# One fused transformer block with a mixture of experts on one core: a block's work spread over four periods instead of three, attention by q times k, a residual added on TensorE

## The reference, cut to what matters

```
x  = attn_q_x                                   # [16, 512, 256]
z  = layernorm(x);  xn = layernorm(z) * ln1_w + ln1_b
q, k, v = xn @ wq + bq, xn @ wk + bk, xn @ wv + bv      # each 16 heads of 16
fq, fk = elu(q) + 1, elu(k) + 1
kv   = einsum('bhnd,bhne->bnde', fk, v)         # per token 16 x 16
qkv  = einsum('bhnd,bnde->bhne', fq, kv)
den  = einsum('bhnd,bnd->bhn', fq, fk.sum(heads))
a    = (qkv / (den + 1e-6)) @ wo + bo;  y = z + a
x1   = x + y + (gelu(layernorm2(y) @ fc_w + fc_b) @ proj_w + proj_b)
t    = layernorm(x1)
top 2 of 8 experts by t @ gate_w.T, weights by softmax
out  = x1 + shared(t) + sum over the two experts of w_e * expert_e(t)
       # shared and each expert: (silu(t @ g) * (t @ u)) @ down, 384 wide
```

## Time and profile before

| | |
|---|---|
| median of 3 runs | 1912.48 us (1909.49 to 1914.32) |
| the profiled execution's own time | 1909.86 us |
| its span | 1908.1 us |
| mean granted TensorE clock in it | 0.935 of full |
| busy over the span: PE, DVE, POOL, ACT | 91%, 67%, 67%, 40% |
| busy from 700 to 800 us: PE, DVE, POOL, ACT | 94.05, 92.16, 88.52, 49.94 us of 100 |

### The profile page before, as it was taken

One profiled execution on the slowest core, in us unless ns is written; L12 is line 12 of the kernel. 1 busy time (PEld: TensorE's weight loads), 2 busy tenths in 40 slices (PEclk: granted clock), 3 DMA queues, 4 the chain that ended last, 5 costly groups with the idle time before them and its releaser, 6 DMA issues.

```text
span 1908.1 us, 25917 instructions
## 1 busy us (share of the span) xinstructions
PE 1739.2 (91%) x7160; PEld 1247.1 (65%) x7161; DVE 1275.3 (67%) x2291; ACT 772.7 (40%) x1518; POOL 1270.5 (67%) x749
## 2 busy tenths in 40 slices
PE   3489998999999999998999899797999999999997
PEld 1255665555656655665566566555888888888886
DVE  7999898988988989889889899613222222222221
ACT  2245455354454453544544534431333322333222
POOL 4877888888888888889888888802333333333333
PEclk8699898898998988989989889888999999999999
DMA  5001110110101101101011010106777777677674
GB/s 188 27 29 44 45 45 23 44 38 28 44 11 44 44 22 44 42 25 44 15 41 44 22 44 34 41 4 187 157 162 163 162 158 157 161 163 164 158 155 90
DMA packets 87130, 148.57 MB, mean 78 GB/s; under 512 B 8640, under 2 KB 71872, under 8 KB 86720
## 3 DMA queue, kind: packets, MB, share of 16 engines
q1 hardware_dynamic: 60512, 112.58, 18.9%
q0 software_dynamic: 26592, 35.67, 11.2%
HBM read 101.79 MB, written 48.56 MB: 79 GB/s over the span
## 4 chain that ended last, share of the span: by engine, by line
PE 47%; POOL 26%; DVE 14%; issue 8%; ACT 3%; DMA 1%; POOLq 0%; DVEq 0%; SPq 0%; ACTq 0%
POOL prod_pool L464 10%; PE p_b L1362 10%; PE p_b L1373 10%; PE p_q L1362 7%; PE p_b L1301 6%; DVE prod L838 4%; POOL prod_pool L537 3%; PE p_v L1362 3%; POOL prod_pool L482 3%; PE p_b L1222 3%; POOL rows_sorted L501 3%; POOL prod_pool L520 3%; DVE prod L863 2%; PE p_b L1270 2%; DVE kvT L846 2%
## 5 line engine op out<-in xcount | busy, mean ns | idle before, releaser
L577 POOL DMA_INDIRECT out_rows<-prod_pool,prod x142 | 220.9, 1555 | 384.3 <-ACT prod_pool L756 353.8
L464 POOL TENSOR_TENSOR prod_pool<-prod_pool 128x544 f32<-128x544 f32 (+4 forms) x240 | 400.0, 1667 | 18.8
L1270 PE MATMUL p_b<-bT,fc_sb 128*128 128x512 f32 x512 | 225.6, 599 | 12.1 <-ACT bT L683 12.1
L1222 PE MATMUL p_b<-proj_sb,hid 128*128 128x256 f32 x1024 | 230.5, 379 | 0.0
L846 DVE TENSOR_REDUCE kvT<-prod 128x128 f32<-128x2048 f32 x96 | 219.5, 2286 | 2.7
L838 DVE TENSOR_TENSOR prod<-p_q,v_dve 128x4096 f32<-128x4096 f32 x48 | 211.9, 4415 | 0.0
L1222 PEld LDWEIGHTS p_b<-proj_sb,hid 128*128 128x128 f32 x1024 | 189.6, 190 | 27.7 <-issue 0.5
L1301 PE MATMUL p_b<-bT,sgup_sb 128*128 128x512 f32 x384 | 206.5, 695 | 0.0
L1362 PE MATMUL p_b<-prod,exp_up 128*128 128x256 f32 x840 | 187.1, 379 | 0.0
L1270 PEld LDWEIGHTS p_b<-bT,fc_sb 128*128 128x128 f32 x512 | 96.5, 191 | 131.8 <-issue 108.1
L876 DVE TENSOR_REDUCE qkv<-prod 128x204 f32<-128x3264 f32 x48 | 170.4, 3550 | 4.0 <-DVE rs_a L808 3.2
(11 more groups left out here) (164 smaller groups left out, 2867.0 us busy)
## 6 DMA issues: line engine op xcount, KB each, us to landing
exp_up<-in_experts SPq DMA_DIRECT2D x71, 768.0 KB, 4.7
prod<-rows_sorted SPq DMA_DIRECT2D x71, 260.0 KB, 2.8
xin<-in_x SPq DMA_DIRECT2D x16, 512.0 KB, 3.4
xres<-in_x SPq DMA_DIRECT2D x16, 512.0 KB, 3.6
out_rows<-x SPq DMA_DIRECT2D x16, 512.0 KB, 3.3
exp_dn<-in_experts SPq DMA_DIRECT2D x8, 384.0 KB, 5.5
out_rows<-prod_pool,prod POOLq DMA_INDIRECT x142, 3.8
rows_sorted<-rows SPq DMA_DIRECT2D x2, 1040.0 KB, 6.7
```

What stands on the lines that cost most here:

```text
L464: done(g.tensor_tensor(prod_pool[:, at:at + n * w], prod_pool[:, at:at + n * w], prod_pool[:, at + n * w:at + 2 * n * w], ALU.add))
L577: pool.indirect_dma_start(out=out[:, :], out_offset=bass.IndirectOffsetOnAxis(ap=tok_i[j][:, a:a + 1], axis=0), in_=yg[j][:, a * D:(a + 1) ...
L1222: ins = t_.matmul(o, src[:, k, t * P:(t + 1) * P], w[:, k, :], start=k == 0, stop=bias_at is None and k == chunks - 1)
L1270: ins = t_.matmul(bnk[:], fc_sb[:, k, f * P:(f + 1) * P], bT[:, k, :], start=k == 0, stop=k == KC - 1)
```

## The change

The pipeline gets a stage more. Under `stages(c)` a body now has `core` (block c, attention), `stage_b` (block c-1: wo, LayerNorm 2, gelu layer), `stage_c` (block c-2: LayerNorm 3, router, shared expert's up products, scatter) and `stage_d` (block c-3: shared down product, store). The program runs periods 0 to 18 instead of 0 to 17. The hardware loop holds two periods a round (c = 4 to 13), because `rows` and `x1` now alternate between two buffers.

- On TensorE the router and the whole shared expert of block c-2 (6 up products, and the down product of c-3) stand ahead of `hT` and the gelu layer of block c-1. The up products use two PSUM banks instead of three.
- Attention first multiplies q with k (scores 16x16 for each token, `products_1`, `sums_1`), sums the scores to the denominator (`totals`), then multiplies scores with v (`products_2`, `sums_2`). Every product has 4096 elements for 16 heads. VectorE does tiles 1 and 3 whole and half of the heads of tile 2; GpSimd tile 0 whole and the other 8 heads of tile 2, in one go (`heads`).
- The scores stay in the tile's q and k bank, and so do denominators and small statistics; `pq_free` for tile 1, 2 and 3 is given after the division, not after the second product. For tile 3 that is after `attn_ready`.
- POOL's addition of `xmid` to `xres` is gone. TensorE adds `xmid` in PSUM by a product with the identity in `to_tokens` (`plus`).
- A few values of four or eight numbers (`first2`, `gap_1`, `shift_c`) pass through PSUM.

The diff, cut to its core: the sizes, TensorE's body from `x3T` to `hT`, the added product, VectorE's two new steps, the first half of VectorE's body, and GpSimd's `heads`.

```
-DVE_HEADS = 12
-POOL_HEADS = HEADS - DVE_HEADS
+SPLIT = 2
+POOL_HEADS = 8
...
             def body(c, j):
...
+                if stage_c:
+                    transpose_block(rows[j % 2], (p_b0, p_b1), x3T_psum,
+                                    lambda t: wait(pe, rows_ready, TPB * (c - 2) + t + 1))
                 if core:
                     project_x(c, 2, "P")
+                if stage_c:
+                    logits(c)
+                if stage_d:
+                    down(c)
                 if stage_b:
+                    if stage_c:
+                        wait(pe, ln2_var, c)
+                        shared_up(c)
+                    if core:
+                        project_x(c, 3, "P")
+                    if stage_c:
+                        ranks(c)
+                        wait(pe, up_taken, 2 * HCH * (c - 1))
                     transpose_block(hnorm, (p_b2, p_b3), hT_psum,
...
+                    if plus is not None:
+                        t_.matmul(o, ident[:], plus[:, t, :], start=False, stop=False)
...
+            def products_1(u):
+                done.sync()
+                n = own_heads(u)
+                done.later(v.tensor_tensor(
+                    prod[:, 0:n * HH].rearrange("p (h g d) -> p h g d", h=n, g=HEADS),
+                    p_qk[u % 2][:, 0:n * HD].rearrange("p (h d) -> p h d", h=n).unsqueeze(2)
+                    .to_broadcast([P, n, HEADS, HD]),
+                    eqk[u % 2][:, D:2 * D].rearrange("p (g d) -> p g d", d=HD).unsqueeze(1)
+                    .to_broadcast([P, n, HEADS, HD]), ALU.mult))
+            def sums_1(u, lo, hi):
+                done.sync()
+                done.later(v.tensor_reduce(
+                    p_qk[u % 2][:, lo * HEADS:hi * HEADS],
+                    prod[:, lo * HH:hi * HH].rearrange("p (a d) -> p a d", d=HD), AX.X, ALU.add))
...
             def body(c, j):
...
                 if core:
+                    features(c, 1)
+                    products_1(1)
+                if stage_c:
+                    shift_3(c)
+                if core:
+                    sums_1(1, 0, half)
+                if stage_b:
+                    residual_1(c)
+                if core:
+                    keep_scales(c)
+                    if more:
+                        ln1_stats(c + 1)
+                if stage_b:
+                    scales_b(ln2_std, ln2_scale, c)
+                if core:
+                    sums_1(1, half, HEADS)
+                    totals(1, den_1[:, 0:HEADS])
+                    products_2(c, 1, False)
+                    if more:
+                        ln1_scales(c + 1)
+                if stage_c:
+                    choose(c, j)
+                if core:
+                    done.sync()
+                    guard(den_1[:, 0:HEADS])
+                    sums_2(1)
+                    inverse(den_1[:, 0:HEADS])
+                    if more:
+                        dve.wait_ge(ln1_scale, c + 2)
+                    wait(dve, attnT_psum, KC * c)
+                    features(c, 2)
+                    done.sync()
+                    done.later(divide(0, 0, qkv[1][:], den_1[:, 0:HEADS]))
+                    if stage_c:
+                        dve.wait_ge(chosen_ready, c - 1)
+                    release(c, 1)
+                    products_1(2)
...
             def heads(c):
+                wait(pool, feat_ready, 4 * c + SPLIT + 1)
+                own = slice(HEADS, HEADS + POOL_HEADS)
+                features = eqk[SPLIT % 2]
+                announce(pool, scores(features[:, (HEADS - POOL_HEADS) * HD:D], by_head(features[:, D:2 * D]), POOL_HEADS),
+                         share_qk_used, c + 1)
+                announce(pool, halve(flat(s_pool[:, own, :])), pool_s, c + 1)
+                announce(pool, mixed(s_pool[:, own, :], v_dve[SPLIT % 2][:].rearrange("p e g -> p g e"),
+                                     POOL_HEADS), share_v_used, c + 1)
+                announce(pool, halve(flat(qkv_pool[:, own, :])), pool_qkv, c + 1)
```

More of the change, by code:

```diff
@@ L383, in body, with store @@
                         sp.dma_start(exp_dn[:, e, :], experts[e, :, EXU:EXW]).then_inc(experts_in, 16)
[L384 to L394, removed]
+                if stage_d and (core or stage_b):
+                    store(c, j)
+            def store(c, j):
+                wait(sp, out_ready, c - 2)
+                sp.dma_start(out_blk[bass.ds(c - 3, 1)].rearrange("b p t d -> p (b t) d"), x1[(j + 1) % 2][:]
+                             ).then_inc(out_stored, 16)
+            periods(sp, body)
             sp.wait_ge(pads_at, 1)
@@ L679, in body @@
                     rsqrt(rs_a[:, 0:2], sq_a[:], ln1_log, ln1_std, c + 2)
+                if stage_c and stage_b:
+                    table(ACT.Silu)
+                    take_shared(c)
+                    table_exp_ln()
+                    wait(act, gap_ready, c - 1)
+                    a.activation(gap_e[:], gap[:], ACT.Exp).then_inc(gap_exp, 1)
+                if core:
+                    take_qkv(c, 3)
                 if stage_b:
@@ L714, in body @@
                 if stage_b:
-                    wait(act, gap_ready, c)
-                    a.activation(gap_e[:], gap[:], ACT.Exp).then_inc(gap_exp, 1)
-                    table(ACT.Silu, 2)
-                    take_shared(c, range(3, 2 * HCH))
+                    scales_3(c)
             act.wait_ge(pool_const, 3)
@@ L730, in _ @@
             take_qkv(0, 1)
[L731 to L736 removed]
+            periods(act, body)
             def take_gT(k, j):
@@ L1050, in body @@
-                if stage_b:
-                    place(c)
-                if core and not last:
-                    done.sync()
-                    dve.sem_inc(pq_free, 1)
-                if stage_b:
-                    weights(c)
+                        dve.sem_inc(pq_free, 1)
             dve.wait_ge(pool_const, 4)
@@ L1227, in to_tokens, with body @@
                         ins.then_inc(ready, 1)
-            def body(c, core, stage_b, tail):
-                more = core and (not isinstance(c, int) or c < BLOCKS - 1)
+            def body(c, j):
+                core, more, stage_b, stage_c, stage_d = stages(c)
                 if core:
```

678 lines of the change are left out of this document (344 added, 334 removed).

## The result

| | before | after |
|---|---|---|
| median | 1911.2 us (1909.49 to 1914.32, 4 runs) | 1930.36 us (1928.72 to 1933.22, 4 runs) |
| ratio | | 1.010, 95% interval 1.008 to 1.012 |
| the profiled execution: own time, span | 1909.86, 1908.1 | 1928.72, 1926.6 |
| mean granted TensorE clock | 0.935 | 0.958 |

The change makes the kernel 1.0% slower. The forecast was 1880 us with 0.75 for faster: wrong in sign, and the range ended at 1930.

A forecast was written before the change was run, and what follows sets the result against it. No engine full: a ring of waits from TensorE's up products through ScalarE and GpSimd to VectorE. Loop -34 (73.1 against 75.9 us, 12 periods), start -4, last attention -7, tail +15: -30, so 1880 us; range 1845 to 1930.

The forecast's parts named there:

- step 3: VectorE's stretch from `features` of tile 1 to the release of tile 1's bank: 29.2 us, before 23.7.
- `shift_3` +0.25: Time that adding `shift_3` to VectorE's stretch before the release of tile 1's bank would cost: 0.25 us a period.
- the cast of L948: VectorE's 4-number SBUF-to-SBUF write, 843 ns, held up by the port shared with GpSimd; reading PSUM was counted at 0.17.
- the ring: Longest cycle of waits among the engines per steady period: 73.1 us against 75.9; chance 0.55 as laid out.
- steps 1 and 2: From attention's end: handoff and TensorE's projection of tile 1, 3.2 us, then ScalarE's take, 1.3 us.
- step 4: TensorE from tile 3's projection through hT, gelu product and `proj`, with residual products +1.7: 35.6 us; TensorE ready 1.5 early.
- The clock falls every period: Rival: many short TensorE waits halve its clock for about 10 us a period; period 76.6, about 1929 us; chance 0.19.
- DVE alone bounds: Rival: TensorE's stretch is shorter than thought, so VectorE sets a 71.3 us period; 1858 us; chance 0.14.
- POOL bounds: Rival: GpSimd's 16-head products slow by 2.5 us each, so it takes 74.5 a period; about 1897 us; chance 0.06.
- The moves cancel: Rival: longer handoffs and a router step delaying tile 3's projection give period 75.4; 1909 us; chance 0.06.
- The tail: After the last attention: gelu product starts at 28.3 us, +14.2; residual products +1.7, router about -1; in all +15.
- wo "as before": In the tail, wo ends about 6.4 us after the last attention: transposes, a copy and 3.9 of wo.

The follow-up runs named there:

- e4: Changed kernel with shift_3, still with two SBUF inputs, moved ahead of products_1(1); 1951.7 us, ratio 1.020 to the kernel before.
- e5: Changed kernel with one-input shift_3, plus one more 4-wide two-SBUF-input instruction behind it whose output nobody reads; 1933.4 us, ratio 1.011 to the kernel before.
- e1: Changed kernel with shift_3 copying rs_c into PSUM first, then multiplying that with mv_c from SBUF; 1883.8 us, ratio 0.986 to the kernel before.
- e2: Changed kernel with TensorE's projection of tile 2 moved ahead of the x3T transposes, shift_3 unchanged; 1928.9 us, ratio 1.009 to the kernel before.
- e6: Changed kernel with one-input shift_3, GpSimd adding xmid to xres again and the identity products gone; 1864.2 us, ratio 0.974 to the kernel before.
- e10b: Changed kernel with one-input shift_3 and weights product, GpSimd residual, and 9 and 3 unread TensorE fill products in the last two periods; 1860.7 us, ratio 0.974.
- e12: Changed kernel with one-input shift_3 and weights product, GpSimd residual, and 4 and 1 unread TensorE fill products in the last two periods; 1858.7 us, ratio 0.972.
- e3: Changed kernel with one-input shift_3 and TensorE's projection of tile 2 ahead of the x3T transposes; 1905.5 us, ratio 0.996 to the kernel before.

## Why the prediction was wrong

**The step that failed** is one number in step 3: "`shift_3` +0.25". It measured 2.83 + 0.16 = 3.0. I took L841's kind as the price and did not look where the operands lie. The diff shows it: `mv_c` and `rs_c` are both in SBUF, and only the output goes to PSUM. What the runs measured: this instruction with two SBUF inputs, issued while GpSimd is in a product, ends when that product ends (2.83, 3.67, 2.56 us at three phases, within 0.04 us of the end in each of twelve periods of the changed kernel, e4 and e5); with one of the inputs in PSUM it takes 0.16. So the engines of this kernel do not meet only at semaphores, as I wrote at the start: VectorE stood here for GpSimd without one. The Trainium skill, "SBUF — State Buffer", Who interferes with whom, states just this in the same list that I cited for the cast of L948: two SBUF inputs contend with a GpSimd instruction that reads SBUF. I applied the page to the instruction that went and not to the one that came. The detour through PSUM for L948 did pay (the copy L986 takes 0.17); that of `shift_c` was on the wrong side of its instruction, at its output instead of an input.

**What followed from it.** In the period shown, the release of tile 1's bank came 3.7 us late (2.75 for the instruction, 1.5 at L841 behind TensorE's half clock, less 0.6 elsewhere). Over the ring the period grew by 3.3 in the mean (76.24 against 72.93). In the four periods without a wait at L841 the release is at 31.2 to 31.3 us and the period 75.5 to 75.7, so 2.7 of the 3.3 are the hold of VectorE, which e5 shows to be enough by itself (75.6 to 75.9); the other periods add up to 1.7 more through TensorE's half clock, 0.6 in the mean.

**The rest of the ring was right.** Without the stall (e1), attention's end to `features` of tile 1 took 4.5 us (steps 1 and 2: 4.5); from there to tile 3's projection 28.8 (29.5 with its handoff); to the second residual bank 35.7 (35.3); to attention's end 4.0 (3.8). Sum 72.9 against 73.1, and 1884 us against 1880. The slack that step 4 gave TensorE was too large: it waited 0.40 us for the release and not 1.5, so a little more work on it would have made it the bound. In the profiled execution of e1 the loop and the first periods were together 3 us shorter than in my sum and the tail 4 longer, so part of the nearness of the total is luck.

**The rivals.** "The clock falls every period" gave 1929 us, the time that was measured, and does describe part of the trace; but its cause, many short waits or two PSUM banks, was not the cause here: in e1 such waits (0.35, 0.40, 1.2, 1.5 us) and the same banks leave the clock at 1.00. In the changed kernel it fell behind the wait of some 3 us that L966 made. The number was right by luck. But the rival's mechanism is not refuted in general: in e2 the clock fell in eleven of the twelve periods, and no wait of TensorE in its loop was longer than 1.9 us. "DVE alone bounds" was nearly reached by e6 (71.7 against 71.3), and there GpSimd bounded as well. "POOL bounds" was wrong for the changed kernel: it waited 7.2 us a period, and its strided products took 4.88 each (4.9 taken). "The moves cancel" needed longer handoffs; they were not longer.

**The tail.** +19.2 against +15. The gelu product started 32.6 us behind the last attention, not 28.3: TensorE stood 4.11 us for the last attention (2.92 in the kernel before, where wo stayed at full clock), and transposes, wo and down ran wholly or partly at half clock, about 4 us in sum. e10b and e12 show the same work at full clock. I took wo "as before" without asking what TensorE does ahead of it in the new order. That 2.92 us left the clock up and 4.11 did not is what the traces show; no run varied that wait by itself.

## What to carry to other kernels

Price an added instruction by the row whose operands lie in the same memories and whose neighbour engine is as busy, not by its size: 4 numbers cost 2.8 us here, and moving one operand to PSUM won 2.4% of the kernel. When a stall shows in a trace, compare its end with the ends of the other engines' instructions before asking the semaphores. And a fallen clock is often the second event: undo the wait ahead of it first, and ask of the work that you want to move into a wait what it covers now.

## What the runs showed of the hardware

- The VectorE instruction with two SBUF inputs paid for the whole rest of GpSimd's instruction, up to 3.67 us, and GpSimd nothing: L549 took 3.43 us with L966 waiting and 3.45 without.
- TensorE's granted clock fell behind idles of 3.0 and 4.1 us, and in e2 and e3 behind idles of 1.23 and 1.16 us with 9.7 and 8.5 us between them; in e1 idles of 1.22 and 0.35 us at nearly the same places left it at 1.00. The length of one idle does not decide: before the change the clock fell behind 2.30 us in the loop and not behind 2.92 in the tail, and in e5 and e4 it fell behind waits of 3.0 and 3.7 us for the release in some periods and not in others. Which pattern of idles decides was not settled.
